# Scaling half of the mask rows on ScalarE, and Newton corrections in three steps, in a two-layer attention and MLP kernel

## What is computed

```python
x = x + attention0(layernorm(x), ctx)          # 16 heads, latent, with rotary tables
x = x + ffn0(layernorm(x))                     # emulated FP8: scale by abs-max, cast, w_fc, relu^2, scale, cast, w_proj
x = x + attention1(ctx, ctx, mask, key_mask, qc_score=layernorm(x))
x = x + ffn1(layernorm(x))                     # rmsnorm, value path, rmsnorm, gated MLP, routed per token

def attention1(q, k, attn_mask, key_padding_mask, qc_score):
    scores = (q @ Wq.T + bq) @ (k @ Wk.T + bk).T * 64 ** -0.5 * qc_score
    mask = attn_mask[None] | key_padding_mask[:, None]
    return softmax(where(mask, -inf, scores))
```

## Time and profile before

| | us |
|---|---|
| median of three runs | 420.69 |
| profiled execution | 420.42 |
| its span, first to last instruction | 418.6 |
| TensorE busy | 388.5 (93%) |
| VectorE busy | 309.6 (74%) |
| ScalarE busy | 215.5 (51%) |
| GpSimd busy | 182.9 (44%) |
| mean granted TensorE clock | 0.975 |

### The profile page before, as it was taken

One profiled execution on the slowest core, in us unless ns is written; L12 is line 12 of the kernel. 1 busy time (PEld: TensorE's weight loads), 2 busy tenths in 40 slices (PEclk: granted clock), 3 DMA queues, 4 the chain that ended last, 5 costly groups with the idle time before them and its releaser, 6 DMA issues.

```text
span 418.6 us, 6243 instructions
## 1 busy us (share of the span) xinstructions
PE 388.5 (93%) x2114; PEld 259.8 (62%) x2119; DVE 309.6 (74%) x686; ACT 215.5 (51%) x576; POOL 182.9 (44%) x172
## 2 busy tenths in 40 slices
PE   8799899999999999999999999988779797699997
PEld 8565656666666566566555677834155454588886
DVE  5796688866667576767677665476989998997673
ACT  1533646465656555655555785336959532464140
POOL 2545464646554655456555311843920051054200
PEclk9999999999999999999999999988969999989999
DMA  7645020030020010000400000500000000000001
GB/s 257 219 137 212 1 86 16 1 102 2 2 100 2 23 80 1 2 0 2 139 2 0 2 0 28 153 0 2 1 0 2 0 0 2 0 1 2 25 27 51
DMA packets 9087, 17.54 MB, mean 42 GB/s; under 512 B 2144, under 2 KB 6944, under 8 KB 8160
## 3 DMA queue, kind: packets, MB, share of 16 engines
q1 hardware_dynamic: 9056, 17.14, 12.1%
HBM read 16.09 MB, written 1.05 MB: 41 GB/s over the span
## 4 chain that ended last, share of the span: by engine, by line
PE 61%; DVE 25%; ACT 8%; issue 4%; DMA 1%; POOL 0%; DVEq 0%; ACTq 0%
PE bank L1318 7%; PE bank L1442 7%; PE bank L1436 6%; PE bank L1411 6%; PE bank L1320 6%; PE bank L1319 5%; PE bank L1424 5%; DVE rot_up L876 3%; PE bank L1396 3%; ACT prob L620 3%; DVE tail_all L1140 2%; PE bank L1341 2%; DVE relu L1026 2%; ACT probT L611 2%; PE bank L1670 2%
## 5 line engine op out<-in xcount | busy, mean ns | idle before, releaser
L456 POOL TENSOR_TENSOR prob<-prob,rinv 128x512 f32<-128x512 f32 x64 | 66.5, 1040 | 106.3 <-DVE rinv L934 106.3
L620 ACT ACTIVATE prob<-bank,negmax 128x256 f32<-128x256 f32 x128 | 60.0, 479 | 40.6 <-DVE negmax L929 40.6
L929 DVE TENSOR_REDUCE negmax<-bank 128x2 f32<-128x512 f32 x64 | 41.2, 686 | 25.0 <-PE bank L1411 24.6
L611 ACT COPY probT<-bank 128x512 f32<-128x512 f32 x64 | 37.8, 590 | 19.6 <-PE bank L1424 19.5
L451 POOL TENSOR_TENSOR rot_low<-rot_low,rot_up 128x512 f32<-128x512 f32 x32 | 40.8, 1275 | 11.3 <-DVE rot_up L876 11.3
L876 DVE TENSOR_TENSOR rot_up<-bank,cb 64x512 f32<-64x512 f32 x64 | 44.1, 689 | 0.9
L1318 PE MATMUL bank<-xnT,w 128*128 128x512 f32 x96 | 42.0, 438 | 2.1 <-DVE xnT L852 1.7
L1424 PEld LDWEIGHTS bank<-ca,prob 128*128 128x128 f32 x256 | 30.5, 141 | 18.8 <-issue 16.1
L874 DVE TENSOR_TENSOR rot_low<-bank,cb 128x512 f32<-128x512 f32 x32 | 22.0, 689 | 25.6 <-PE bank L1320 25.6
L1424 PE MATMUL bank<-ca,prob 128*128 128x128 f32 x256 | 38.9, 275 | 1.7 <-ACT probT L611 1.1
L436 POOL TENSOR_TENSOR c_y<-c_ve,minus_half 128x4 f32<-128x4 f32 (+1 forms) x9 | 9.8, 1088 | 64.6 <-DVE c_ve L833 52.7
(11 more groups left out here) (213 smaller groups left out, 798.7 us busy)
## 6 DMA issues: line engine op xcount, KB each, us to landing
blobs<-in_blob SPq DMA_DIRECT2D x7, 1024.0 KB, 6.2
xs<-in_x SPq DMA_DIRECT2D x2, 512.0 KB, 4.0
xn<-in_w_fc_t SPq DMA_DIRECT2D x1, 1024.0 KB, 5.0
ctxT<-in_w_proj_t SPq DMA_DIRECT2D x1, 1024.0 KB, 5.6
out<-qk SPq DMA_DIRECT2D x8, 128.0 KB, 1.7
cb<-in_const_b SPq DMA_DIRECT2D x1, 768.0 KB, 8.1
blobs<-in_w_gate SPq DMA_DIRECT2D x1, 704.0 KB, 4.5
blobs<-in_w_up SPq DMA_DIRECT2D x1, 704.0 KB, 5.9
```

The lines of the kernel that those rows point to most:

```text
L456: pool.tensor_tensor(p[:], p[:], rinv[:, n % PROBS, :].unsqueeze(2).to_broadcast([P, 2, S]), ALU.mult).then_inc(normed, 1)
L611: act.copy(probT[n % 2][:].rearrange("p a s -> p (a s)"), pT[:]).then_inc(probsT_copied, 1)
L620: ins = act.activation(prob[n % PROBS][:, st, :], pS[n % 2][:, st * S:(st + 1) * S], ACT.Exp, bias=negmax[:, n % 2, st:st + 1], accum_out= ...
L929: dve.tensor_reduce(negmax[:, n % 2, :], pS[n % 2][:].rearrange("p (a s) -> p a s", a=2), AX, ALU.max, negate=True).then_inc(max_ready, 1)
```

## The change

ScalarE takes the scaling of the mask rows for batches 2 and 3, as two instructions of 128x512, before its wait for `d_small`; it waits for the masks' two DMAs first. GpSimd, for these two batches, waits for a new semaphore in place of the scaling and its in-order wait, and adds. Batches 0 and 1 are as before.

`newton` has three steps: -0.5 * y * y, times ve, and (that + 1.5) * y. The first and the last are scalar_tensor_tensor instructions, and the tensor_scalar of L825 is gone.

```diff
@@ block.gpsimd
             def mask_rows(b):
                 mb = mbias[:, 2 * b:2 * b + 2, :]
                 kb = ktmp[:, b * S:(b + 1) * S].unsqueeze(1).to_broadcast([P, 2, S])
-                in_order(pool.tensor_scalar(mb, mA[:], MASKED, None, ALU.mult))
+                if b < 2:
+                    in_order(pool.tensor_scalar(mb, mA[:], MASKED, None, ALU.mult))
+                else:
+                    pool.wait_ge(mask_scaled, b - 1)
                 return pool.tensor_tensor(mb, mb, kb, ALU.add)
@@ block.scalar
+            act.wait_ge(d_mask, 32)
+            for b in range(2, B):
+                act.activation(mbias[:, 2 * b:2 * b + 2, :], mA[:], ACT.Copy, scale=MASKED).then_inc(mask_scaled, 1)
             act.wait_ge(d_small, 16)
             for i in range(2):
                 for c in range(2):
@@ block.vector
                 ve, y, w = of[0][:, lo:hi], of[1][:, lo:hi], c_t[:, lo:hi]
                 dve.wait_ge(power_ready, n)
-                in_order(dve.tensor_tensor(w, y, y, ALU.mult))
+                in_order(dve.scalar_tensor_tensor(out=w, in0=y, scalar=-0.5, in1=y, op0=ALU.mult, op1=ALU.mult))
                 in_order(dve.tensor_tensor(w, w, ve, ALU.mult))
-                in_order(dve.tensor_scalar(w, w, -0.5, 1.5, ALU.mult, ALU.add))
-                in_order(dve.tensor_tensor(o[:, lo:hi], y, w, ALU.mult))
+                in_order(dve.scalar_tensor_tensor(out=o[:, lo:hi], in0=w, scalar=1.5, in1=y, op0=ALU.add,
+                                                  op1=ALU.mult))
```

More of the change, by code:

```diff
@@ L292, in build @@
         vo_ready, vo_copied = sem("vo_ready"), sem("vo_copied")
-        bvb_ready, d_gate = sem("bvb_ready"), sem("d_gate")
+        bvb_ready, d_gate, mask_scaled = sem("bvb_ready"), sem("d_gate"), sem("mask_scaled")
         wgu_rounded, wgu_low = sem("wgu_rounded"), sem("wgu_low")
```

## The result

Over 17 executions of each kernel in turn, before has a median of 419.14 us and after 416.58 us (414.69 to 420.34). The ratio is 0.9925 with a 95% interval of 0.9896 to 0.9955: 0.75% faster, which on 419.14 us is about 3.1 us (the two medians lie 2.6 us apart). The interval reaches from 0.45 to 1.04%, so that it is faster is sure, and that it passes 0.5% is not. 3.0 us were forecast on 420.69, a ratio of 0.9929. The measured median lies at the low end of the range, and not because the change brought more: two of the first three executions of before were high (420.69 and 421.07), and its own median over 17 is 1.5 us lower.

The account below looks back on a forecast made before the run. The chain was taken as TensorE, then VectorE from 286 to 366 us, partly held by GpSimd, then TensorE. Mask rows 2.0 us plus corrections 1.0 us gave 3.0 us off: 417.5 us, range 416.2 to 419.0.

Parts of the forecast that it names:

- GpSimd holds the products: At the scale for the hidden rows, GpSimd's SBUF reads block VectorE's two 128x1 products; ending GpSimd earlier gives 2.0 us.
- The transpose is in time, by 0.2 us. From there [...] all one chain that moves as a whole: Behind the two products, TensorE's transpose ends before the reduce needs it, and the rest through ScalarE to VectorE shifts together.
- The sum: 2.0 us from the mask rows plus 1.0 us from the Newton corrections, 3.0 us together; forecast chance 74%.
- part one: Mask rows: GpSimd drops two scalings and ends 3.1 us earlier, so the two held VectorE products shrink, 2.0 us together.
- what is late next: The check of what holds the reduce once the products are short; it named the transpose, in time by 0.2 us.
- at most 0.2 us: Effect of TensorE's low clock behind its gap near the scale, since VectorE bounds that stretch.
- ScalarE's work costs nothing: Two scalings near 274 us, taken as 1.3 us, fit ScalarE's 3.13 us idle time: nothing on the chain.
- Calls 4 to 8, 0.20 us each: Newton corrections at 328 to 358 us, in VectorE's own stretch, each lose one step: 1.0 us together.
- Call 3 gives nothing: Correction after the reduction `pad`, ready at 280.15 us while TensorE releases ScalarE only at 280.49: no gain.
- Calls 9 to 11: nothing: Newton corrections beside or ahead of TensorE work without a gap, after about 366 us: no gain.
- The clock's rivals: TensorE's clock after 366 us: no fall, 1.7 us more gained, 415.8 us, 7%; or a longer low clock, 4%.
- The rival on the other side: After 366 us TensorE's 1.2 GHz lasts about 10.6 us more, costing 5.3 us: 422.7 us; chance 4%.

Follow-up runs that it names:

- e1: Mask half of the change alone, Newton corrections in four steps as before, against the kernel before: 417.19 us, ratio 0.9944.
- e3: Kernel before with the scale's two products written as tensor_scalar, one SBUF tensor input each, GpSimd untouched: 417.67 us, ratio 0.9958 to before.
- e5: Kernel after, but GpSimd scales batch 2 again and ScalarE only batch 3: 417.14 us, ratio 0.9947 to before.
- e11: Kernel after with three tiny in-order memsets on VectorE at the very start: 416.10 us, ratio 0.9940 to before.
- e12: The kernel of e8 with three tiny in-order memsets on VectorE at the very start: 414.84 us, ratio 0.9917 to before.
- e6: Kernel after with eight more scalings of 128x512 on ScalarE behind the two: 416.52 us, ratio 0.9936 to before.
- e2: Three-step Newton corrections alone, mask rows all on GpSimd, against the kernel before: 418.73 us, ratio 0.9977.
- e4: Kernel after with seven idle TensorE products ahead of the turning of the maxima: 416.51 us, ratio 0.9931 to before.
- e10: The same kernel as e8, run again: 415.85 us, ratio 0.9923 to before.
- e8: Kernel after with eleven idle TensorE products in the MLP's gap and 27 warming products in place of 24: 415.39 us, ratio 0.9897 to before.
- e7: Kernel after with eleven idle TensorE products in the MLP's gap: 416.26 us, ratio 0.9924 to before.
- e9: Kernel after with 27 in place of 24 warming products at the start: ratio 0.9898 to before, without one odd execution.

## Where the prediction was right, and the step that failed

**GpSimd holds the products: right, shown** by e1, e3 and e5 in three ways. 2.0 us were forecast, and with the clock up and the place unchanged the stretch gives 2.3 (4.89 to 2.63). Of the 0.3 beyond, 0.2 are the hand-over through TensorE at full clock, whose copy waits 0.48 us in place of 0.68, and the rest are products of 0.15 us in place of 0.17. The rule of the Trainium skill, page SBUF — State Buffer, section "Who interferes with whom", held in these traces: instructions with two SBUF inputs took 0.38 to 2.00 us and ended within 0.03 us of a GpSimd subtraction, and with one tensor input they took 0.15 to 0.21 us beside the same subtraction.

**"The transpose is in time, by 0.2 us. From there [...] all one chain that moves as a whole": the step that failed.** The sum put nothing between the products and the copy of the scale, and so took the full 2.0 us for part one. In after it gave 1.60 us (4.89 to 3.29). The transpose itself was in time: in e1, where nothing waits, it ends 0.1 us ahead of the reduce. Two other things stood in its place. The reduce waits 0.28 to 0.40 us where the other half of the change has moved the instructions' places (0.49 in after, with TensorE's turn at 0.42 us in place of 0.33). And TensorE's four score products, which I left out of "what is late next", take 2.07 us at half clock and reach to the hand-over. I had given TensorE's low clock behind this gap "at most 0.2 us"; e11 against e12 has 0.6. Before had room for both, since its products held VectorE for 2.4 us. The size went, 0.4 us of 3, and not the mechanism of the hold.

**The sum and the chances.** That the total came out at 3 us all the same is in part luck: call 3, below, gave 0.2 us that I had put at nothing. I also gave 0.79 that the kernel would come out faster by more than the 0.5% that can be told. The interval begins at 0.45%, so that isn't settled. I had taken the forecast's 0.9 us above that line for enough, and single executions of after, 414.69 to 420.34 us, spread over six times as much.

**ScalarE's work costs nothing: right**, at 0.57 us for each scaling, near the lower bound, and with far more cover than I said (e6).

**Calls 4 to 8, 0.20 us each: nearly right.** Call 4 gives 0.20 in e1 to after (19.97 to 19.77), call 8 gives 0.20, calls 5 to 7 give 0.52 in place of 0.60. Where the 0.08 went: `h_tile` 1 to 3 take 1.35 us in after and 1.26 in before. It is 1.35 to 1.36 in each trace of a three-step kernel at normal speed and 1.26 in before, e1 and e3. TensorE's products for them had ended 1.7 us and more before the last of them starts, so TensorE is not the cause; what is stays open. The stretch with call 4 is 20.0 to 20.15 us in e2, e4, e5 and e10 to e12, and not 19.8, and in e3, with four steps, 20.24: there TensorE delivers the first tile of the second product 0.2 us late. In these seven its half clock lasts until 8.7 to 10.6 us behind the copy of the scale; in before, after, e1, e6 and e8, which don't wait, until 7.3 to 7.6 us (e7, at 8.5 us, loses 0.18 us without such a wait). From e12:

```profile
313.43 0.48 DVE L1061 SCALAR_TENSOR_TENSOR xs<-bank,sc,xs 128x256 f32<-128x256 f32 x1 [0.21 <-PE bank L1630]
```

I had taken that VectorE's stretch moves as a whole. Here too TensorE is close behind it.

**Call 3 gives nothing: wrong in 12 of the 13 traces at normal speed.** I read it from the one execution in which TensorE did the projections at half clock (0.50 from 278.5 us). At full clock they end before `pad` is ready, call 3 is on the chain, and it gives 0.2 us: 15.83 us in e1 (and in e3), 15.62 in e2 (and 15.6 in every other three-step kernel). From the chain in after:

```profile
281.46 0.04 issue
281.50 0.18 DVE c_t L829
281.70 0.18 DVE c_t L830
281.90 0.18 DVE rstd L831
```

So in after's profiled execution the terms are 1.6 (part one), 0.2 (call 3), 0.2 (call 4), 0.5 (calls 5 to 7) and 0.2 (call 8), together 2.7 us against 3.0. Where the clock and the places leave part one its 2.3, the same sum would be 3.4.

**Calls 9 to 11: nothing, right.** In after call 10 even waits 0.30 us for its power, since call 9 is faster. Nobody waits for that.

**The clock's rivals.** In the profiled execution of after, the clock did not fall in the MLP, as that rival had it, and that gave 1.1 us and not 1.7. But it is a matter of each execution, not of the change: it falls in e1 to e5 and in e11, and not in e6. I should have given it as the spread of single executions and not as a case of its own. The rival on the other side, a longer half clock in the MLP, did not come; the longest was e3's, 6.8 us of it, which cost 2.1 us.

## What to carry to other kernels

An off-path GpSimd is not free: look where a tiny VectorE instruction takes microseconds, and whether it ends with a GpSimd instruction. Ask also which engine is next in line, and at half clock too. Then either end GpSimd's work before the instruction, and no earlier than needed, or give the VectorE instruction a single SBUF tensor and check that the next one with two does not inherit the hold. When an edit removes instructions from a long program, compare the waits at places that it does not touch: 0.3 to 0.4 us appeared at one here. And read from one profiled execution which call is on the chain only with its granted clock beside it.

## What the runs showed of the hardware

- VectorE's wait at one place of its program appeared with three instructions fewer ahead of it (0.28 to 0.49 us in seven kernels) and went with three memsets (0.04 us in e12). Why is open.
- One execution of e9 took 740.61 us. TensorE's 128x256 products of the attention's context took 722 ns each in it and 379 ns in after; its idle products (128x512, bf16) started 443 ns apart, where at full clock it is 216 and at half clock 427. The views give a granted clock of 1.00 for it, but its trace holds no record of the clock at all, and its page has no row PEclk; each other trace holds four to eight records. So the 1.00 says nothing: TensorE ran near half speed throughout. Nothing in the kernel explains it, and it came once.
- ScalarE took 0.57 us for each scaling of 128x512 from bytes (after), no more than the 0.63 us of its squares over as many floats, where GpSimd takes 1.50.
